# Reordering a fused attention and mixture-of-experts kernel: the head before expert 0 and the leads in the last expert

## The reference, cut to what matters

```
xn  = layernorm(x)                                  # x: 4 x 4096 x 1024, f32
k   = exp(1j * (xn @ Wk) * 10);  v = xn @ Wv        # 16 heads of 64
rot = exp(1j * t * freqs)
pos   = real(cumsum(v * rot) * conj(rot)) / sqrt(t + 1)
assoc = real(cumsum(v * conj(k shifted by 1)) * k) / sqrt(t + 1)
attn  = (pos * gate[:, 0] + assoc * gate[:, 1]) @ Wo
e, w  = argmax, max of softmax(xn @ gate_w)         # 8 experts, one per token
ffn   = w * (gelu(xn @ w1[e] + b1[e]) @ w2[e] + b2[e])
out   = x + attn + ffn
```

## Time and profile before

| | us |
|---|---|
| median of 3 runs | 1130.99 (1130.82 to 1131.71) |
| profiled execution, its time | 1131.58 |
| profiled execution, span of the slowest core (core 1) | 1129.5 |
| spans of the 8 cores | 1120.4 to 1129.5 |
| PE busy | 935.5 (83%) |
| DVE busy | 692.5 (61%) |
| ACT busy | 597.7 (53%) |
| POOL busy | 161.6 (14%) |

### The profile page before, as it was taken

The page is one execution under the profiler, slowest core; times in us unless marked ns, Lnnn a source line. Parts: engine busy times, 40 slices in busy tenths (PEclk is TensorE's granted clock), DMA queues, the critical chain, the costliest instruction groups (busy, mean ns, idle before and its releaser), DMA issues.

```text
span 1129.5 us, 18153 instructions; the slowest of 8 cores (1120.4 to 1129.5 us)
## 1 busy us (share of the span) xinstructions
PE 935.5 (83%) x6296; PEld 609.3 (54%) x6296; DVE 692.5 (61%) x1498; ACT 597.7 (53%) x1014; POOL 161.6 (14%) x184
## 2 busy tenths in 40 slices
PE   3756599899899999989878988898889874598683
PEld 2223466566566676566555656565656552354352
DVE  5726535665445334779966998899989992132151
ACT  4354488769965884577437634863486332121000
POOL 0000121001112111121112101210121110221111
PEclk9876599999999999999899998998999986899887
DMA  8999889998999999999999999999999999999983
GB/s 211 228 199 201 182 144 182 168 185 144 165 160 158 180 180 160 157 170 173 160 172 166 172 158 182 167 166 157 170 173 170 157 159 199 199 238 226 213 221 93
DMA packets 123774, 199.64 MB, mean 177 GB/s; under 512 B 4757, under 2 KB 70693, under 8 KB 123680
## 3 DMA queue, kind: packets, MB, share of 16 engines
q0 software_dynamic: 107056, 151.64, 90.5%
q1 hardware_dynamic: 16624, 46.80, 13.1%
HBM read 321.18 MB, written 17.90 MB: 300 GB/s over the span
## 4 chain that ended last, share of the span: by engine, by line
PE 43%; DMA 30%; DVE 11%; issue 7%; ACT 6%; POOL 1%; DVEq 0%; SPq 0%; ACTq 0%; POOLq 0%
DMA ring<-w 13%; PE yb L944 13%; PE wb L627 13%; PE wb L889 10%; DMA yg<-ys,gidx 9%; DMA wos<-wo 4%; PE yb L412 3%; DVE pp L736 3%; DMA ys<-xsr 1%; PE wb L588 1%; DVE pp L741 1%; DVE st L346 1%; DVE pp L743 1%; DVE pp L760 1%; DVE pp L756 1%
## 5 line engine op out<-in xcount | busy, mean ns | idle before, releaser
L889 PE MATMUL wb<-xsT,ring 128*128 128x288 bf16 x2048 | 279.2, 295 | 44.2 <-DMA ring<-w 29.8
L944 PE MATMUL yb<-hT,ring 128*128 128x288 bf16 x2048 | 278.9, 291 | 23.1 <-ACT yT L959 16.2
L889 PEld LDWEIGHTS wb<-xsT,ring 128*128 128x128 bf16 x2048 | 204.2, 101 | 115.4 <-issue 50.8
L944 PEld LDWEIGHTS yb<-hT,ring 128*128 128x128 bf16 x2048 | 202.1, 100 | 92.9 <-issue 32.1
L321 POOL DMA_DIRECT2D ring<-w x128 | 106.0, 832 | 750.7 <-PE yb L944 358.5
L899 ACT ACTIVATE hT<-wb,cfs 128x288 bf16<-128x288 f32 x256 | 118.8, 500 | 131.7 <-PE wb L889 128.6
L674 DVE COPY cs<-bnd 128x2 f32<-128x2 f32 x64 | 10.8, 169 | 168.1 <-ACT cs L658 160.0
L627 PE MATMUL wb<-xT,wks 128*128 128x512 bf16 x384 | 95.9, 395 | 5.3 <-ACT hT L899 5.3
L795 PE MATMUL wb<-wos,z 128*128 128x512 bf16 x256 | 68.0, 414 | 32.6 <-DVE resf L804 18.3
L627 PE MATMUL wb<-xT,wvs 128*128 128x512 bf16 x384 | 92.3, 384 | 0.0
L656 ACT ACTIVATE cs<-cs 128x512 f32<-128x512 f32 x64 | 40.3, 630 | 79.3 <-DVE cs L650 79.2
(11 more groups left out here) (152 smaller groups left out, 1242.9 us busy)
## 6 DMA issues: line engine op xcount, KB each, us to landing
ring<-w POOLq DMA_DIRECT2D x128, 1024.0 KB, 26.0
xt<-xown SPq DMA_DIRECT2D x16, 512.0 KB, 7.4
xt<-xfh SPq DMA_DIRECT2D x16, 512.0 KB, 9.6
resf<-xown SPq DMA_DIRECT2D x16, 512.0 KB, 13.5
out<-resf SPq DMA_DIRECT2D x16, 512.0 KB, 9.5
xr<-xnb SPq DMA_DIRECT2D x16, 256.0 KB, 7.7
yg<-xr SPq DMA_DIRECT2D x16, 256.0 KB, 8.1
ys<-xsr SPq DMA_DIRECT2D x7, 576.0 KB, 10.9
```

Of the source, the lines that this page charges most:

```text
L889: fn = lambda e, kt=kt, b=b, a=a, k=k: e.matmul(b[:, 0:CAP], ring[k][:, (kt % 4) * DM + a * P:(kt % 4) * DM + (a + 1) * P], xsT[:, kt * CA ...
L944: fn = lambda e, d=d, kc=kc, k=k: e.matmul(yb[d][:, 0:CAP], ring[k][:, (kc % 8) * CH + d * P:(kc % 8) * CH + (d + 1) * P], hT[:, kc * CAP: ...
```

## The change

Head: two xn32 buffers take turns (the second lies over ring buffers 4 and 5, so that their first feeds wait for the last logits); the ACT copy of the logits moves out of `logits` into `take_logits`, one iteration later, and the turn one more; half tiles 0 to 3 are normalized and turned in iterations 11 to 15; routing goes 8 + 8 tiles instead of 12 + 4, the first part inside the loop; Wk and Wv are loaded at i = 4 and 7, the ring's pieces 0 to 3 at i = 1, 9, 11, 13; the rotor's halves come at i = 3 and 7, the sines behind the second route; kv(0) and unit 1 run ahead of expert 0. The lists of units move accordingly. Last expert: eight yg buffers (four lie over xT), four gathers ahead, sums three tiles behind, no item before step 10 of stage 1, items until step 8 of the second half of stage 2, `fetch_last` at step 16 and `last_rows(0)` at step 24 of it.

```diff
-NRES = 13
-NYG = 4
+NRES = 11
+NYG = 8
...
-    xn32 = sb("xn32", KT * CH, F32, hT_off)[0]
+    xn32 = [sb("xn32%d" % k, KT * CH, F32, o)[0]
+            for k, o in enumerate((hT_off, ring_off + 8192 * (NRING - 2)))]
...
+    yg = yg + [sb("yg%d" % (4 + k), DM, BF16, xT_off + 2048 * k)[0] for k in range(NYG - 4)]
...
-    V.op(lambda e: e.memset(ap(rm, 0, [[NLT * NE, P], [12, NE]]), 0.0), t)
-    V.op(lambda e: e.memset(ap(rm, 12 * NE, [[NLT * NE, P], [4, NE]]), 0.0), t)
+    V.op(lambda e: e.memset(ap(rm, 0, [[NLT * NE, P], [8, 2 * NE]]), 0.0), t)
...
-    x_order = [(xown, i) for i in range(NLT)] + [(xfh, i) for i in range(NLT)]
+    x_order = [(xown, i) for i in range(12)]
+    for i in range(4):
+        x_order += [(xfh, i), (xown, 12 + i)]
+    x_order += [(xfh, i) for i in range(4, NLT)]
...
-        if i0 + n in (4, 8, 12):
-            xn32_free[0] = t_l
-        t_c = S.op(lambda e: e.activation(lgT[0:NE, c], b[0:NE, c], AF.Identity),
+        xn32_free[i0 // 4 % 2] = t_l
+        return i0, n, c, t_l
+
+    def take_logits(i0, n, c, t_l):
+        t_c = S.op(lambda e: e.activation(lgT[0:NE, c], yb[3][0:NE, c], AF.Identity),
...
-            fetch_rows(i + 2, y_d)
-            if i > 0:
-                add_rows(i - 1)
+            fetch_rows(i + 4, y_d)
+            if i > 2:
+                add_rows(i - 3)
             if i == NLT - 1:
-                add_rows(i)
+                for k_ in range(i - 2, NLT):
+                    add_rows(k_)
...
-                d_ys.tok(), d_z.tok(), t_gi[0], yg_t.get(i - NYG), *fx_free)
+                d_ys.tok(), d_z.tok(), t_gi[0], yg_t.get(i - NYG), *fx_free,
+                *buf_free[0])
...
     for i in range(NLT):
         k, t = st_t[i]
+        f = i - 11
         t_nf = norm(k, xnf[i % 2], t, *nf_free[i % 2])
         pull()
+        if 0 <= f < 4:
+            fh_begin(f)
         begin(i + 1)
         got = turn_own(i, t_nf)
         t_b = rows_own(i, t_nf)
         nf_free[i % 2] = (t_b, got[1][2])
+        if 0 <= f < 4:
+            fh_end(f)
         end(i + 1)
-        if turning:
-            turn_logits(*turning)
-            turning = None
+        if taken:
+            turn_logits(*taken)
+            taken = None
+        if summed:
+            taken = take_logits(*summed)
+            summed = None
         if i - 1 in groups and i < NLT - 1:
-            turning = group(i - 1)
+            summed = group(i - 1)
         evs[i] = put_own(i, got)
-        if i in (1, 4, 7, 9):
+        if f > 0:
+            turn_rows(f - 1)
+        if i in (1, 9, 11, 13):
             feed(loaded[-1][1])
+        if i == 4:
+            wkv(wks, wk)
+        if i == 7:
+            t_wkv[0] = wkv(wvs, wv)
+        if i in (3, 7):
+            rotor(i // 4 * 4, 4)
         if i == 11:
-            G.dma(d_wkv, lambda e: e.dma_start(w3(wks), wsrc(wk)), loaded[-1][1])
-        if i in (4, 8):
-            rotor(i - 4, 4)
-        if i == 12:
-            rotor_sines()
-    route(0, 12)
-    turning = group(14)
-    late = group(NLT - 1)
-    turn_logits(*turning)
-    turn_logits(*late)
-    for i in range(12):
+            route(0, 8)
+    group(14)
+    late = group(NLT - 1)[3]
+    for i in range(8):
         lines_up(i, t_pos[i])
-    t_wkv[0] = G.dma(d_wkv, lambda e: e.dma_start(w3(wvs), wsrc(wv)))
-    fh_norm(0, 1)
-    route(12, 4)
-    for i in range(12, NLT):
+    turn_logits(*take_logits(12, 4, slice(0, CH), late))
+    route(8, 8)
+    rotor_sines()
+    t_u0 = kv(0)
+    for i in range(8, NLT):
         t_m = lines_up(i, t_pos[i])
     take_lists(t_m)
     load_xs(0)
-    turn_rows(0)
-    turn_rows(1)
-    fh_norm(2, 3)
     weigh()
...
+    rneg(0, t_u0)
     for _ in range(NRING - 4):
-        feed()
-    turn_rows(2)
-    turn_rows(3)
+        feed(lg_t[NLT - 1])
+    unit(1)
     turn_xs(0)
     fh_norm(4, 5)
...
     first = {
-        0: mix(US(0, 4), [L(4), L(5, 6, 7), L(6), L(7, 8, 9)]),
-        1: US(12, 16) + [L(12), U(16), L(13, 14, 15), U(17)],
-        2: mix(US(24, 28), OS(0)),
-        3: US(34, 38),
-        4: US(41, 45),
-        5: US(49, 53),
-        6: US(57, 61),
-        7: W(0, 8),
+        0: mix(US(2, 6), [L(4), L(5, 6, 7), L(6), L(7, 8, 9)]),
+        1: US(12, 16) + [L(12), U(16), L(13, 14, 15)],
+        2: US(22, 24) + mix(US(24, 28), OS(0)),
+        3: US(32, 36),
+        4: US(40, 44),
+        5: US(48, 52),
+        6: US(56, 60),
+        7: W(0, 6),
     }
     second = {
-        0: US(4, 8) + [L(8), L(9, 10, 11), U(8), L(10), U(9), L(11, 12, 13), U(10), U(11)],
-        1: [L(14), U(18), L(15), U(19), two, weights_last] + US(20, 24),
-        2: US(28, 34),
-        3: US(38, 40) + OS(1) + US(40, 41),
-        4: US(45, 48) + OS(2) + US(48, 49),
-        5: US(53, 56) + OS(3) + US(56, 57),
-        6: US(61, 64) + [load_wo, U(64), load_x4],
-        7: W(8, 16),
+        0: US(6, 8) + [L(8), L(9, 10, 11), U(8), L(10), U(9), L(11, 12, 13), U(10), U(11)],
+        1: [L(14), U(17), L(15), U(18), two, weights_last] + US(19, 22),
+        2: US(28, 32),
+        3: US(36, 40) + OS(1),
+        4: US(44, 48) + OS(2),
+        5: US(52, 56) + OS(3),
+        6: US(60, 64) + [load_wo, U(64), load_x4],
+        7: W(6, 16),
     }
...
-            fix.append((2, lambda: (fetch_rows(0, y_d), fetch_rows(1, y_d))))
+            fix.append((2, lambda: [fetch_rows(i, y_d) for i in range(4)]))
...
-        stage1(e_, spread(first[e_], NCT, fix))
+        lead = 0 if e_ < NE - 1 else 10
+        plan = {lead + k: v for k, v in spread(first[e_], NCT - lead).items()}
+        for k, x in reversed(fix):
+            plan.setdefault(k, []).insert(0, x)
+        stage1(e_, plan)
...
-            stage2(e_, spread(second[e_], NCT, [(NCT + 6, fetch_last),
-                                                    (NCT + 20, lambda: last_rows(0))]))
+            stage2(e_, spread(second[e_], NCT + 8, [(NCT + 16, fetch_last),
+                                                        (NCT + 24, lambda: last_rows(0))]))
```

More of the change, by code:

```diff
@@ L120, in build_program @@
     vb = [sb("vb%d" % k, CH, BF16)[0] for k in range(NCS)]
-    xT, _ = sb("xT", KT * CH, BF16)
+    xT, xT_off = sb("xT", KT * CH, BF16)
     wos = sb("wos", KT * DM, BF16, final_off)[0]
-    assert at[0] - final_off >= 2 * KT * DM + 4096 * NRES
+    assert xT_off - final_off >= 2 * KT * DM + 4096 * NRES
     resf = [sb("resf%d" % i, DM, F32, final_off + 2 * KT * DM + 4096 * i)[0]
             for i in range(NRES)]
-    ring = []
-    ring_off = at[0]
+    ring, ring_off = [], at[0]
     for k in range(NRING):
@@ L143, in build_program @@
     z = [sb("z%d" % k, KT * CH, BF16)[0] for k in range(4)]
-    yg = [sb("yg%d" % k, DM, BF16)[0] for k in range(NYG)]
+    yg = [sb("yg%d" % k, DM, BF16)[0] for k in range(4)]
     fxn = yg[2:]
+    yg = yg + [sb("yg%d" % (4 + k), DM, BF16, xT_off + 2048 * k)[0] for k in range(NYG - 4)]
     poh = [sb("poh%d" % i, CAP, BF16, r1 + 24576 + 2 * CAP * i)[0] for i in range(NLT)]
@@ L413, in logits @@
                 b[0:NE, c], gws[:, kt * NE:(kt + 1) * NE],
-                xn32[:, kt * CH + c.start:kt * CH + c.stop],
+                xn32[i0 // 4 % 2][:, kt * CH + c.start:kt * CH + c.stop],
                 start=(kt == 0), stop=(kt == KT - 1))
@@ L540, in weigh @@
     def weigh():
-        for i0, n in ((0, 12), (12, 4)):
+        for i0, n in ((0, 8), (8, 8)):
             t = V.op(lambda e, i0=i0, n=n: e.tensor_tensor(
@@ L566, in build_program, with fh_begin @@
     x_ready = {}
-    def fh_norm(*fs):
+    def fh_begin(*fs):
         for f in fs:
@@ L577, in fh_norm @@
             pull()
+    def fh_norm(*fs):
+        fh_begin(*fs)
+        fh_end(*fs)
     fh_k, nf_t = {}, {}
@@ L1033, in build_program @@
     end(0)
-    evs, turning = {}, None
+    evs, summed, taken = {}, None, None
     groups = {3: (0, 4), 7: (4, 4), 11: (8, 4), 14: (12, 3), 15: (15, 1)}
```

16 lines of the change are left out of this document (9 added, 7 removed).

## The result

The changed kernel takes 1162.04 us (median of 4 runs) beside 1131.35 us for the kernel before on the same chip (4 runs): ratio 1.0266, interval 1.0247 to 1.0284. The forecast was 1111. The profiled execution took 1161.88 us with a span of 1160.1 us on core 6; core 1, which the rows of before show, has 1149.9 (1129.5 before).

A forecast was written before the change was run, and what follows sets the result against it. The prediction took a chain of small steps to bound the head, PE experts 0 to 2, transfers and DVE later; span 1129.5 + 1.8 - 13.8 + 5.8 - 13.3 = 1110.0 us, forecast 1111, range 1097 to 1126.

The forecast's parts named there:

- Part 1 and 2: Head, own-tile loop and the stretch behind it: expert 0 starts at 133.7 instead of 131.9, +1.8 us.
- I take the two to cancel: Head loop, first two groups: up to 4.8 us gained per group offset by the rotor's 6.1 us on DVE.
- Part 3: Experts 0 and 1: two kv units fewer each, at -6.9 us per expert, -13.8 us in all.
- Part 4: Experts 4 to 6: one outs more for DVE puts expert 7's start near 920.2, +5.8 us.
- 23 steps of 14.0 us: DVE's z rows from 615.4 to 936.5 in the kernel before; the forecast counted 24 such steps after the change.
- (d): Slower rival: DVE decides, the last z and expert 7's start come 14 us later; 1135 us, chance 0.09.
- Part 5: Expert 7: less PE work owed after the last weight piece and no last wait on fetch_last, -13.3 us.
- The 17 us from the last transposes to the end stay: Tail behind expert 7: its 17 us were forecast to remain unchanged.
- a microsecond for outs that land beside: Expert 7's end: allowance of one microsecond for outs landing beside, within the -13.3 us.
- The median of 38.3 us for pieces: Expert 7: time from issue to landing, putting the last weight piece, issued at 1057.3, in by about 1095.
- (a): Fast rival: the head's loop keeps its gain, -12 instead of +1.8 us; 1097 us, chance 0.12.
- (b): Fast rival: transfers have headroom, expert 7's 171 us become 16 fewer; 1095 us, chance 0.05.

The follow-up runs named there:

- e2: Kernel before with the last expert's part of the diff alone; 1126.48 us beside 1125.37, ratio 0.9989.
- e3: Changed kernel with the last expert of the kernel before; times spread from 1156.9 to 1200.4 us, so no ratio.
- e7: Kernel before with the last expert's changes, but twelve yg buffers and gathers eight tiles ahead; ratio to before 0.9995.
- e6: Changed kernel with the fourth stage 2 unit of experts 3 to 5 at step 33 instead of 28; ratio to before 1.011.
- e14: Changed kernel with five units in stage 1 of expert 3 and a unit again behind the own tiles in experts 3 to 5; ratio to before 1.0030.
- e9: Kernel before with unit 33 moved from expert 2 to 3, unit 40 kept behind the own tiles; ratio 0.9999.
- e10: Kernel before with units 32 and 33 moved from expert 2 to 3, unit 40 kept behind the own tiles; ratio 1.0029.
- e4: Changed kernel with the unit lists of the kernel before from expert 1 on, expert 0 keeping ten units; ratio to before 0.9993.
- e15: Changed kernel with the fourth stage 2 unit of experts 3 to 5 at step 50, own tiles at 53 to 62; ratio to before 1.0177.

## Why the prediction was wrong, step by step

**Part 1 and 2 (expert 0 at 133.7, +1.8): wrong, +6.2 on core 1 and +8.4 as a mean.** On core 1 the second route starts at 117.3, 5.3 us later than before, where -3.2 was forecast; from there to the gather it is 4.6 us more (forecast 4.0), and from the gather to expert 0 3.8 less. So the loop is what failed. The groups of four now start at 33.9, 57.4, 83.3 and 107.9, against 27.3 and 49.0. The rotor, no longer beside the logits, leaves PE idle ahead of the group's last tile, and in iterations 11 to 14, which take two x tiles each, these came late:

```profile
32.03 1.94 PE L387 MATMUL wb<-cfs,xnf 128*128 128x128 f32 x8 [6.31 <-DVE xnf L362]
...
55.52 1.94 PE L387 MATMUL wb<-cfs,xnf 128*128 128x128 f32 x8 [7.00 <-DVE xnf L362]
```
```profile
91.34 0.69 DVE L349 BATCH_NORM_STATS2 st<-xt 128x6 f32<-128x512 f32 x1 [2.54 <-DMA xt<-xown]
97.82 0.69 DVE L349 BATCH_NORM_STATS2 st<-xt 128x6 f32<-128x512 f32 x1 [1.95 <-DMA xt<-xfh]
101.75 0.69 DVE L349 BATCH_NORM_STATS2 st<-xt 128x6 f32<-128x512 f32 x1 [2.32 <-DMA xt<-xown]
```

"I take the two to cancel" was the weak point: 6.6 us later at the first group, not 0. By the DMA view Wv is in near 87, before these three waits, so it isn't shown that Wk and Wv delay the tiles. Behind the loop DVE waits 2.61 us for the last of the sines, and its L480 stands behind it at 126.6. While the gather (128.4) waited for the lists, DMA had little to do (120:132, before first, then changed; the earlier trace rows has the lists of before at 117.2):

```profile
120.00:132.00 12.00, 4.05 (x42) 3.66 (x43) 7.22 (x26) 4.83 (x8) 3.57 (x4) 0.50 0.87 182
```
```profile
120.00:132.00 12.00, 8.16 (x48) 3.74 (x47) 7.32 (x34) 7.67 (x11) 3.05 (x3) 0.78 0.13 32
```

**Part 3 (-13.8 by expert 3's start): the two units came off, the time did not.** Experts 0 and 1 are 10.0 and 7.2 us shorter (means), more than 6.9 each; but expert 2, with ten units as before, is 9.3 longer, and expert 3 starts where it did (+0.5). From expert 0's start to expert 3's it is 333.7 us instead of 341.6 (means): 7.9 of the 13.8, inside the bound "0 and -13.8", and the head's 8.4 took them. Length times rate of the stretches says why not more: 56.8 MB before and 57.0 now, and 57.0 MB in 336 us are 170 GB/s, the rate that I had read as this mix's limit. I had priced expert 1's reserve (157 of 170) and given the same to the sum of three. That transfers hold this stretch is argued from the rate, and 170 is no hard edge: pairs of runs on one chip, with the old head and the new (e2 and e3, e7 and e6), differ by 10.7 and 10.4 us from expert 0's start to expert 3's, and e14 passes the stretch at 173 GB/s on core 1. The Trainium skill's "HBM Reference" (Specifications) gives a core about 358 GB/s when both cores of a domain stream, which would leave reserve there. No run bears that out: over their spans the profiles show 292 to 303 GB/s of HBM traffic.

**Part 4 (+5.8 by expert 7's start): this is the step that failed.** It costs +37.2 between the starts of experts 3 and 7. I took "23 steps of 14.0 us" from the z of unit 40 to the last and carried them on as if the step belonged to the outs. It doesn't: it is 13.42 us and, before, two long steps at each border (25.0 and 21.6 at the first, near 16 each at the others), and what stands at the border depends on where the unit is that issues the outs; in the change it is one step of 27.6 to 28.6. Nor did the sum have a term for expert 3, which takes 126.6 us instead of 111.2. Against e14, whose experts 3 to 7 take 456.2 us, 29.9 of the +37.2 are the lists without a border unit (9.8, 10.2 and 8.7 of it in experts 4, 5 and 6); the other 7.3 are there in e14 as well, which also has units 32 and 33 in expert 3. I counted units per expert and never asked, for the last unit of an expert, which later one issues its outs, though `unit` says so in five lines. Rival (d), "DVE decides", had the engine right, but priced it as one outs more (14 us): e9 and e10 show that one or two outs moved, with the border unit in place, cost 0 and 0.3%. What was forecast of ACT, that it stands behind rneg, is right and not the cost.

**Part 5 (-13.3): the debt went as forecast, the end did not come.** From expert 7's start to the last W2 it is 11.6 us less in e2 and 12.8 less in e4, beside the 12.6 of the forecast. "The 17 us from the last transposes to the end stay" failed: gather, sum, store and `fetch_last` follow the last piece, and the tail is 9 us longer; e2's whole is -0.1% with an interval across zero. In the change itself (28.1 us later at the end than before, means), 1115.3 to 1132.9 shows the same:

```profile
1114.78 0.65 PE L957 MATMUL yb<-hT,ring 128*128 128x288 bf16 x4 [2.57 <-DMA ring<-w]
...
1132.86 1.29 PE L1012 MATMUL wb<-cbs,yT 128*96 128x128 bf16 x8 [11.27 <-DVE resf L1020]
```

I had allowed "a microsecond for outs that land beside". The median of 38.3 us for pieces held (39.2), and I used it for pieces alone; the gathers in the same queue take 59.

**Range and chances.** 1097 to 1126 with 0.10 for slower. Of the rivals on the fast side (a) rested on the head and (b) on reserve in the transfers, and neither came; the slower one, (d), was priced by a count, 1135 beside the measured 1162.

What stays open: how the 0.3% of e10 and e14 splits between the later first outs and the steps of 15 to 16 us; why the first border is longer in the kernel before; whether transfers hold experts 0 to 2 and the end, which is argued and not shown; and what the own tiles' loads in e15 cost apart from the gap. The body of unit 39 issued without unit 40 (the direct cure of the border with the new lists) was not tried.
